# Four graph layers on one core: the order of copy and clear of PSUM banks in the counts

## The chip, the cores and the metric

One NeuronCore of a Trainium2 chip runs one program. The metric is the device time of one execution in microseconds (us). The kernel before was timed three times; one further execution was recorded by the hardware profiler.

## The reference

The program computes four residual graph layers on 6250 nodes of 128 features and 200000 edges, sorted by target. Each layer is fed with `h = relu(layernorm(x))` and adds its result to x:

```
x = x + GIN(h)        # h + sum of h[src] over edges into dst, then two dense layers
x = x + attention(h)  # 8 heads, scores with edge features, softmax per target, then norm
x = x + SAGE(h)       # mean of h[src] over edges into dst, two dense layers
x = x + linear(h)     # sum of edge_weight * h[src], one dense layer
```

Layers one and three sum features over the edges. The kernel does that as a dense product with a matrix of counts: entry (source, target) is the number of edges between the two nodes. The targets are drawn as 6250 times the square of a uniform number, so that low node numbers get many edges and high ones few. Building the matrix of counts is the stage that the change touches.

## The kernel before, in words

The order of the whole is: tables of edges, the counts (`build_counts`), layer one, layer two with the building of the weighted matrix beside it, layers three and four. Each stage ends with a barrier of all engines.

In the counts the 6272 targets (49 blocks of 128) are cut into 784 windows of eight targets. The sums of a window stand in one PSUM bank, 128 partitions by 8 x 49 = 392 numbers. There are eight banks; window w uses bank w mod 8. The edges stand in chunks of 128, and a visit is one chunk taken for one window; there are 2352 visits. Per visit:

- VectorE (`hots`, L676 through `one_hots`) compares keys with a counting row and makes two one-hot matrices, for eight visits per pair of instructions, into a ring of 24 visits (`ba_mov`, `ba_sta`).
- TensorE (`visit`, L713) multiplies the two and adds the product onto the window's bank. The matmul does not reset the bank (`start=False`), so the bank has to be zero before a window's first visit. TensorE waits on `s_clear` for a number read from a table (window plus a constant), and on `s_hot` for the one-hots. Its loop's body holds three groups of eight visits; ahead of each group it loads eight registers.
- ScalarE (`evict_counts`) takes the windows by pairs. It waits on `s_vis` until the pair's last visit is done, copies both banks into the stage in SBUF (L737, `ba_stage`), and clears banks by an ACTIVATE with scale 0 (`clear_pair`, L672), which adds 2 to `s_clear`. Eight pairs are a block; behind them ScalarE issues the DMA of the block to `adj_d` (L743). There are two stage buffers. The loop's body holds two blocks, and a last block stands behind the loop. At the start of a block eight ends of pairs are loaded into registers (`pair_ends`), and `s_store` is waited for.

The copy adds 1 to `s_evict`, and a clear waits for `s_evict` before it overwrites the banks that the copy read. `start` clears all banks once and gives `s_evict` and `s_clear` their first values. Beside the counts GpSimd and SyncE move terms for the attention (L811, L813), and VectorE takes the norm's statistics of x behind its last one-hots.

The weighted matrix is built later by the same class (`evict_weights`): there one bank of 392 is copied (L768), waited for (L769) and cleared (L770, recorded as L665) at a time.

Of the kernel before, what the change touches and what calls it, by code (L numbers as in the profile page):

```python
# [26 lines left out]
WPB = P // WN  # L27
# [30 lines left out]
BANKS = 8  # L58
# [561 lines left out]
class Build:  # L620
# [105 lines left out]
    def evict_counts(self):  # L726

        nc, c, act = self.nc, self.c, self.nc.scalar
        half = WPB // 2

        def block(b, par, turn):
            ends = self.pair_ends(b)
            act.wait_ge(self.s_store[par], 16 * turn + 1)
            for k in range(half):
                act.wait_ge(self.s_vis, ends[k] + self.ring)
                out = self.stage[:, par, :].rearrange("p (h d) -> p h d", d=P)[:, :, 2 * k * WN:2 * (k + 1) * WN].rearrange("p h (t d) -> p t h d", t=2)
                act.copy(out, self.pair_of_banks(2 * k % BANKS).rearrange("p t (h d) -> p t h d", d=WN)).then_inc(self.s_evict, 1)  # L737
                if k:
                    act.wait_ge(self.s_evict, b * half + k + 1)
                    self.clear_pair(2 * (k - 1) % BANKS)  # L740
            act.wait_ge(self.s_evict, b * half + half + 1)
            self.clear_pair((WPB - 2) % BANKS)
            act.dma_start(c.adj_d[bass.DynSlice(b, 1), :, :].rearrange("a p n -> (a p) n"), self.stage[:, par, :]).then_inc(self.s_store[par], 16)  # L743
        with act.Fori(0, NB // 2) as i:
            block(2 * i, 0, i)
            block(2 * i + 1, 1, i)
        block(NB - 1, 0, NB // 2)
        act.wait_ge(self.s_store[0], 16 * (NB // 2 + 1) + 1)
        act.wait_ge(self.s_store[1], 16 * (NB // 2) + 1)
# [1627 lines left out]
```

## Time and profile before

| | us |
|---|---|
| median of 3 runs | 5554.05 |
| lowest, highest | 5548.2, 5557.44 |
| the profiled execution's own time | 5533.22 |
| its span | 5531.4 |
| TensorE matmuls busy | 4526.3 (82%) |
| VectorE busy | 3188.8 (58%) |
| ScalarE busy | 1789.2 (32%) |
| copies of the counts (L737, 392) | 316.8 |
| clears of the counts (L672, 396) | 328.0 |

The span is from the first to the last recorded instruction. Busy times are sums of durations; where two instructions of an engine overlap, the overlap is counted once in the stretches but the durations of single groups are added up. In the timelines an instruction that waited has the idle time and its releaser in brackets.

### The profile page before, as it was taken

The page shows a single profiled execution, that of the slowest core. Times are in us where ns is not written, and L with a number is a line of the kernel's source. Part 1 is how long each engine was busy: PE and PEld are TensorE (multiplying, and loading weights), DVE is VectorE, ACT ScalarE, POOL GpSimd, SP SyncE. Part 2 cuts the span into 40 slices and gives each one's busy share as a digit, 9 for nine tenths or more (in the row PEclk, how much of TensorE's full clock was granted, in tenths as well). Part 3 has the DMA queues.
Part 4 walks back from the last instruction along what each step waited for, and adds up shares of the span by engine and source line. Part 5 has one row for each costly group of instructions (what it writes and reads, how often), then busy time and mean ns, then how long its engine had stood idle before and what let it go on. Part 6 is the DMA issues. An engine that isn't in the chain of part 4 may idle for free. (4 is left out here: it accounts for less than half of the span.)

```text
span 5531.4 us, 87976 instructions
## 1 busy us (share of the span) xinstructions
PE 4526.3 (82%) x25332; PEld 3174.1 (57%) x25333; DVE 3188.8 (58%) x4531; ACT 1789.2 (32%) x3407; POOL 2014.9 (36%) x1926
## 2 busy tenths in 40 slices
PE   6888665565899968888888888888884399999999
PEld 4656332222788844554555455555553388888888
DVE  6323988877211058889998989898985710000000
ACT  2433267889200030112333344455552400001000
POOL 0320026300000007777777777777774400000000
PEclk9989999988999999999999999999995599999999
DMA  8885467755766643445555556666665366669998
GB/s 185 171 155 132 112 220 274 289 232 253 305 279 273 273 144 84 116 135 141 158 159 162 173 179 179 195 200 193 199 205 166 135 280 279 279 255 296 300 293 264
DMA packets 736267, 1150.51 MB, mean 208 GB/s; under 512 B 310041, under 2 KB 659421, under 8 KB 717343
## 3 DMA queue, kind: packets, MB, share of 16 engines
q1 hardware_dynamic: 461057, 653.45, 34.7%
q10 hardware_dynamic: 211504, 349.71, 18.0%
q0 software_dynamic: 63600, 146.16, 10.7%
q8 instruction: 38, 0.62, 0.0%
q14 instruction: 68, 0.56, 0.0%
HBM read 762.49 MB, written 393.26 MB: 209 GB/s over the span
## 5 line engine op out<-in xcount | busy, mean ns | idle before, releaser
L1505 POOL DMA_INDIRECT at_qg<-q_d,at_slot x1616 | 1655.7, 1025 | 496.1 <-issue 492.4
L713 PE MATMUL bw_ps<-bw_mov,bw_sta 128*128 128x392 bf16 x7056 | 1575.2, 346 | 22.2 <-issue 8.3
L1548 PE MATMUL at_psk<-at_kp,at_hot 128*128 x4848 | 613.7, 233 | 338.3 <-DVE at_qg L1626 287.0
L713 PEld LDWEIGHTS bw_ps<-bw_mov,bw_sta 128*128 128x128 bf16 x7056 | 630.9, 101 | 372.2 <-issue 103.8
L1548 PEld LDWEIGHTS at_psk<-at_kp,at_hot 128*128 128x128 bf16 x4848 | 435.6, 100 | 684.9 <-issue 477.9
L713 PE MATMUL ba_ps<-ba_mov,ba_sta 128*128 128x392 bf16 x2352 | 513.8, 365 | 317.9 <-ACT ba_ps L672 136.3
L676 DVE TENSOR_TENSOR ba_mov<-iota,key 128x3136 bf16<-128x3136 f16 x294 | 526.8, 1792 | 132.2 <-PE ba_ps L713 127.0
L713 PEld LDWEIGHTS ba_ps<-ba_mov,ba_sta 128*128 128x128 bf16 x2352 | 242.1, 103 | 589.7 <-issue 475.2
L697 DVE TENSOR_TENSOR bw_sta<-bw_raw,kw 128x1024 bf16<-128x1024 bf16 x882 | 557.5, 688 | 0.0
L1054 PE MATMUL l2agg<-tiles,h 128*128 128x256 f32 (+1 forms) x2450 | 525.0, 376 | 22.4 <-PEq L1075 22.4
L1054 PE MATMUL l3agg<-tiles,h 128*128 128x256 f32 (+1 forms) x2450 | 525.8, 377 | 5.2 <-ACT h L915 5.2
L676 DVE TENSOR_TENSOR bw_mov<-bw_ps,lo 128x3136 bf16<-128x3136 f16 x294 | 524.1, 1783 | 4.4 <-PE bw_ps L713 3.7
L1054 PE MATMUL l0agg<-l0adjt,h 128*128 128x256 f32 (+1 forms) x2450 | 525.1, 376 | 0.3 <-ACT h L915 0.3
L768 ACT COPY xall<-bw_ps 128x392 f32<-128x392 f32 x520 | 252.2, 485 | 795.5 <-PE bw_ps L713 765.3
L1054 PEld LDWEIGHTS l2agg<-tiles,h 128*128 128x128 f32 x2450 | 458.3, 191 | 82.5 <-PEq L1075 22.7
L1054 PEld LDWEIGHTS l3agg<-tiles,h 128*128 128x128 f32 x2450 | 458.7, 191 | 65.5 <-issue 5.3
L1054 PEld LDWEIGHTS l0agg<-l0adjt,h 128*128 128x128 f32 x2450 | 457.4, 191 | 60.5 <-issue 0.5
L1626 DVE TENSOR_TENSOR at_qg<-at_qg,at_psk 128x816 f32<-128x816 f32 (+1 forms) x303 | 274.2, 905 | 240.9 <-DMA at_qg<-q_d,at_slot 213.9
L665 ACT ACTIVATE bw_ps<-iota 128x392 f32<-128x392 f16 x788 | 395.0, 502 | 29.4 <-DMA at_tables<-reg_d 4.7
L737 ACT COPY ba_stage<-ba_ps 128x784 f32<-128x784 f32 x392 | 316.8, 818 | 235.4 <-PE ba_ps L713 221.4
L811 POOL DMA_INDIRECT tv_rows<-ed_d,tv_place x101 | 175.7, 1740 | 457.0 <-DMA edv_d<-tv_rows 295.7
L672 ACT ACTIVATE ba_ps<-iota 128x784 f32<-128x784 f16 x396 | 328.0, 839 | 6.4 <-DMA ba_vend<-vend_d 6.4
(412 smaller groups left out, 3811.8 us busy)
## 6 DMA issues: line engine op xcount, KB each, us to landing
adj_d<-ba_stage ACTq DMA_DIRECT2D x49, 3136.0 KB, 9.1
l0adjt<-adj_d SPq DMA_DIRECT2D x23, 6272.0 KB, 17.2
tiles<-adj_d SPq DMA_DIRECT2D x23, 6272.0 KB, 17.3
tiles<-adw_d SPq DMA_DIRECT2D x23, 6272.0 KB, 20.4
adw_d<-xall ACTq DMA_DIRECT2D x65, 1568.0 KB
adw_d<-bw_stage ACTq DMA_DIRECT2D x33, 1568.0 KB
at_rel<-rel_d SPq DMA_DIRECT2D x101, 512.0 KB
at_qg<-q_d,at_slot POOLq DMA_INDIRECT x1616
```

The lines of the kernel that those rows point to most:

```text
L665: self.nc.scalar.activation(self.ps[:, k * 512:k * 512 + WCOL], self.c.iota2[:].rearrange("p n u -> p (n u)")[:, 0:WCOL], ACT.Copy, scale= ...
L672: self.nc.scalar.activation(self.pair_of_banks(k), self.c.iota2[:].rearrange("p n u -> p (n u)").rearrange("p (t n) -> p t n", t=2), ACT.C ...
L676: return self.nc.vector.tensor_tensor(out, self.iota[:, 0:width, :].unsqueeze(1).to_broadcast([P, UV // 2, width, 2]), pairs(keys).unsquee ...
L697: ins = ve.tensor_tensor(self.sta[:, k, v, :, :], self.raw[:, :, :, :], pairs(c.kw[:, 1 + k, bass.DynSlice(t, UV)]).unsqueeze(2).to_broadc ...
L713: ins = pe.matmul(self.ps[:, bass.DynSlice(place, WCOL)], self.sta[:, k, u // 2, :, u % 2], self.mov[:, u // 2, :, u % 2], start=False, st ...
L737: act.copy(out, self.pair_of_banks(2 * k % BANKS).rearrange("p t (h d) -> p t h d", d=WN)).then_inc(self.s_evict, 1)
L768: act.copy(stage[:, (k % half) * WCOL:(k % half + 1) * WCOL], self.bank(k)).then_inc(self.s_evict, 1)
L811: pool.indirect_dma_start(out=rows[:, k, :], out_offset=None, in_=c.ed_d[:, :], in_offset=bass.IndirectOffsetOnAxis(ap=place[:, g:g + 1], ...
L1054: ins = pe.matmul(ps_agg[par][:, 0:n * P], h[:, hi, :], moving[hi], start=hi == 0, stop=hi == NB - 1 and not own_term, skip_group_check=ow ...
L1505: pool.indirect_dma_start(out=qg[:, ring, b, :], out_offset=None, in_=q_d[:, :], in_offset=bass.IndirectOffsetOnAxis(ap=slot[:, ring, b:b ...
L1548: ins = pe.matmul(ps_k[:, at:at + KW], hot[:, par, sum(ROUNDS[:r]) + u, :], kp[:].rearrange("p j k n -> p (j k n)")[:, bass.DynSlice(place ...
L1626: ve.tensor_tensor(q, q, ps_k.rearrange("p (b n) -> p b n", n=512)[:, :, 0:n * KW], ALU.mult).then_inc(s_kr, 1)
```

## The change

The clear of a pair of banks stands behind the copy of that same pair, and waits for that copy. Before, it stood behind the copy of the next pair, and the last pair's clear behind the loop. The wait ahead of the DMA stays.

```diff
--- before.py
+++ after.py
@@ -735,11 +735,9 @@
                 act.wait_ge(self.s_vis, ends[k] + self.ring)
                 out = self.stage[:, par, :].rearrange("p (h d) -> p h d", d=P)[:, :, 2 * k * WN:2 * (k + 1) * WN].rearrange("p h (t d) -> p t h d", t=2)
                 act.copy(out, self.pair_of_banks(2 * k % BANKS).rearrange("p t (h d) -> p t h d", d=WN)).then_inc(self.s_evict, 1)
-                if k:
-                    act.wait_ge(self.s_evict, b * half + k + 1)
-                    self.clear_pair(2 * (k - 1) % BANKS)
+                act.wait_ge(self.s_evict, b * half + k + 2)
+                self.clear_pair(2 * k % BANKS)
             act.wait_ge(self.s_evict, b * half + half + 1)
-            self.clear_pair((WPB - 2) % BANKS)
             act.dma_start(c.adj_d[bass.DynSlice(b, 1), :, :].rearrange("a p n -> (a p) n"), self.stage[:, par, :]).then_inc(self.s_store[par], 16)
         with act.Fori(0, NB // 2) as i:
             block(2 * i, 0, i)
```

## Rows read from the trace of the kernel before

**Rows 1.** The page's costliest groups: mean ns of one, idle before, what ended it.

```profile
L713 PE MATMUL ba_ps<-ba_mov,ba_sta 128*128 128x392 bf16 x2352 | 513.8, 365 | 317.9 <-ACT ba_ps L672 136.3
...
L676 DVE TENSOR_TENSOR ba_mov<-iota,key 128x3136 bf16<-128x3136 f16 x294 | 526.8, 1792 | 132.2 <-PE ba_ps L713 127.0
...
L737 ACT COPY ba_stage<-ba_ps 128x784 f32<-128x784 f32 x392 | 316.8, 818 | 235.4 <-PE ba_ps L713 221.4
...
L672 ACT ACTIVATE ba_ps<-iota 128x784 f32<-128x784 f16 x396 | 328.0, 839 | 6.4 <-DMA ba_vend<-vend_d 6.4
```

**Rows 2.** Timeline behind the counts (start, duration, instruction, idle and releaser).

```profile
1398.25 0.34 ACT L907 ACTIVATE n_rstd<-n_mv,n_eps 128x49 f32<-128x49 f32 x1 [4.74 <-DMA adj_d<-ba_stage]
```

**Rows 3.** Timeline of VectorE at the start of the counts.

```profile
561.60 1.79 DVE L676 TENSOR_TENSOR ba_mov<-iota,key 128x3136 bf16<-128x3136 f16 x1 [3.54 <-PEq L651]
...
563.91 1.78 DVE L676 TENSOR_TENSOR ba_mov<-iota,key 128x3136 bf16<-128x3136 f16 x1
```

**Rows 4.** Busy time by stretch (columns: length, busy and count by engine, clock, DMA).

```profile
716.90:1000.90 284.00, 170.88 (x814) 82.07 (x815) 238.40 (x204) 194.74 (x256) 141.73 (x81) 0.93 0.71 260
1000.90:1377.10 376.20, 230.63 (x996) 105.44 (x994) 294.03 (x250) 333.65 (x448) 29.02 (x17) 0.87 0.60 251
```

**Rows 5.** The same stretches, copies of the counts (L737) alone.

```profile
716.90:1000.90 284.00, 103.33 (x128) 0.93 0.71 260
1000.90:1377.10 376.20, 181.08 (x224) 0.87 0.60 251
```

**Rows 6.** Timeline of ScalarE, one block of the late stretch.

```profile
1110.30 0.82 ACT L737 COPY ba_stage<-ba_ps 128x784 f32<-128x784 f32 x1
...
1113.85 1.53 ACT L737 COPY ba_stage<-ba_ps 128x784 f32<-128x784 f32 x2 [1.26 <-issue]
1115.26 0.85 ACT L672 ACTIVATE ba_ps<-iota 128x784 f32<-128x784 f16 x1
...
1122.40 0.83 ACT L737 COPY ba_stage<-ba_ps 128x784 f32<-128x784 f32 x1
1123.10 0.85 ACT L672 ACTIVATE ba_ps<-iota 128x784 f32<-128x784 f16 x1
1123.86 0.84 ACT L737 COPY ba_stage<-ba_ps 128x784 f32<-128x784 f32 x1
...
1124.93 0.34 ACTq L743 DMA_DIRECT2D adj_d<-ba_stage  x1
1125.31 0.85 ACT L672 ACTIVATE ba_ps<-iota 128x784 f32<-128x784 f16 x1
1126.28 1.53 ACT L737 COPY ba_stage<-ba_ps 128x784 f32<-128x784 f32 x2
```

**Rows 7.** Timeline of ScalarE, first and last copy of the last block.

```profile
1377.12 1.53 ACT L737 COPY ba_stage<-ba_ps 128x784 f32<-128x784 f32 x2 [0.18 <-PE ba_ps L713]
...
1387.44 0.83 ACT L737 COPY ba_stage<-ba_ps 128x784 f32<-128x784 f32 x1
```

**Rows 8.** Timeline of ScalarE in the weighted matrix: copy, wait, clear.

```profile
2402.13 0.48 ACT L768 COPY xall<-bw_ps 128x392 f32<-128x392 f32 x1 [3.22 <-PE bw_ps L713]
2402.65 0.50 ACT L665 ACTIVATE bw_ps<-iota 128x392 f32<-128x392 f16 x1
```

**Rows 9.** Waits up to 1000.9: us in total, times, longest.

```profile
PE ba_ps L713 <- ACT ba_ps L672: 55.9, 52, 2.4
...
DVE ba_mov L676 <- PE ba_ps L713: 45.2, 39, 2.8
```

**Rows 10.** Timeline of TensorE and ScalarE: bursts of visits and a clear.

```profile
601.11 1.56 PE L713 MATMUL ba_ps<-ba_mov,ba_sta 128*128 128x392 bf16 x8 [0.57 <-DVE ba_sta L676]
...
854.42 1.56 PE L713 MATMUL ba_ps<-ba_mov,ba_sta 128*128 128x392 bf16 x8 [1.79 <-issue]
...
860.17 0.83 ACT L672 ACTIVATE ba_ps<-iota 128x784 f32<-128x784 f16 x1
...
861.32 1.56 PE L713 MATMUL ba_ps<-ba_mov,ba_sta 128*128 128x392 bf16 x8 [1.38 <-ACT ba_ps L672]
```


## The prediction

> **What bounds the kernel now.** I began with the chain of waits. It follows back only from the last instruction, stays inside the fourth layer and says nothing of the counts, so it gives no price here. The costliest groups give the four operations of the counts [rows 1]: VectorE builds one-hots (L676), TensorE multiplies them into PSUM (L713), ScalarE copies a pair of banks (L737) and clears it (L672). Nothing else of size runs on these three engines in that stage, and behind it stands a barrier: the last store has to land before the norm's ACTIVATE at 1398.25 [rows 2]. So what the stage gains or loses, the kernel gains or loses one for one. The stage runs from the first one-hot at 561.60 [rows 3] to the last copy at 1387.44 [rows 7].
>
> Busy time by stretch shows that the bound moves [rows 4]. Up to 1000.9 VectorE leads: 238.4 us of 284.0, ScalarE 194.7. Behind it ScalarE leads: 333.7 of 376.2 (89%), VectorE 294.0, TensorE 230.6. The reason is the data: targets are dense at low node numbers, so an early pair of windows needs many visits of TensorE and a late pair only about four, while ScalarE's work for a pair is always one copy and one clear. The copies counted by stretch say it: 128 in 284.0 us, then 224 in 376.2 us [rows 5]. 224 copies are 28 blocks of eight, 13.44 us each.
>
> How near ScalarE is to its limit there is read from its timeline [rows 6]. Copy to clear is 0.70 (1122.40 to 1123.10), clear to copy 0.76 (1123.10 to 1123.86): 1.46 a pair, less than the 0.83 + 0.85 of the two durations, because each instruction starts before the one ahead of it has ended. A block opens with two copies and no clear between them: third copy at 2.17 (1.41 to the first clear at 1115.26, then 0.76), then five more pairs, 2.17 + 5 x 1.46 = 9.47 from first to eighth copy. From the eighth copy to the first of the next block it is 2.42 where the second block of the loop's body follows (1123.86 to 1126.28) and 3.55 across the loop's edge (1110.30 to 1113.85), mean 2.985. Limit now: 12.45 a block against 13.44 measured, so ScalarE idles only 0.99 us a block. A longer ScalarE block can hide there by less than 1 us.
>
> **The change part by part.** Instructions are the same in number: eight copies, eight clears, one DMA per block. What moves is the clear of pair k, from behind the copy of pair k+1 to behind its own copy.
>
> Added: the clear now waits for the copy straight ahead of it to complete, seven times a block more than before (the eighth clear already did). Queued behind this wait on ScalarE are the clear, the next copy and, at the block's end, the DMA; TensorE waits for the clear, the store for the copy. The counts of before don't show this wait between a copy and its clear (the eighth clear stands behind the seventh). The nearest rows are those of the weighted matrix, where the same code order copy, wait, clear stands: copy at 2402.13 for 0.48, clear at 2402.65 [rows 8]. Start to start 0.52, a duration plus 0.04, no overlap. Here that makes 0.82 + 0.04 = 0.86 in place of 0.70. Bounds: 0.70 if the overlap somehow stays; and 1.06 if the wake-up takes the 0.24 that stands between the eighth copy's end (1124.69) and the DMA's issue at 1124.93 [rows 6]. I take 0.86, the row with the same two kinds of instruction.
> The Trainium skill ("ScalarE: Activation LUTs", What ACT_TABLE_LOAD costs) says that back-to-back ACTIVATEs overlap by about 93 ns; the rows show 0.09 behind a clear and about 0.13 behind a copy. By the page's figure the added time a pair would be 0.093 + 0.04 = 0.13 in place of 0.16, and the late sum about 0.03 x 7 x 29 = 6 us smaller.
>
> Clear to next copy stays 0.76: that copy waits only for TensorE. A saturated pair becomes 0.86 + 0.76 = 1.62, first to eighth copy 7 x 1.62 = 11.34.
>
> The block's end: before, the sequencer waits for the eighth copy, queues the clear (1125.31, behind the clear of pair seven), issues the DMA at 1124.93, loads the next ends and sends the next copy at 1126.28, which is 1.59 behind the eighth copy's end. This path starts from the copy's end in both kernels, so 2.42 and 3.55 stand. One clear fewer lies in that window, but it hid beneath the sequencer: no gain. Bound: if the engine set the pace, 0.76 a block could go; I count none, as 1125.31 + 0.76 is 1126.07, ahead of 1126.28. The store's issue keeps its place behind the eighth copy.
>
> Late stretch: 11.34 + 2.985 = 14.325 a block, x 28 = 401.1, against 376.2: +24.9. The last block: 11.34 against 10.32 (1377.12 to 1387.44) [rows 7]: +1.0. Of the 0.99 idle I leave 0.05 a block, +1: TensorE and VectorE wait with full buffers when ScalarE is the slowest, and they get banks earlier. Late total +27.
>
> Removed: the clear of pair k no longer waits for TensorE to finish pair k+1. TensorE needs the banks of pair k for pair k+4. While it still sums pair k+1 and the banks of k are already read, it could go on before only as far as k+3; now k+4 is open too. Where visits are many and ScalarE has time this can shorten waits. Up to 1000.9 TensorE's waits put down to a clear sum to 55.9 us in 52 [rows 9], but a burst of eight visits shows some 0.6 us ahead of it also where nothing but its own pace holds it (0.57 at 601.11, VectorE named) [rows 10]: 55.9 - 52 x 0.6 = 25 us at most. A real case: the clear at 860.17 lasts until 861.00 and the burst starts at 861.32, 1.38 us idle, 0.8 over the usual [rows 10]; the new order would have cleared earlier. Other gaps, such as the 1.79 at 854.42 that is put down to issue [rows 10], have no clear ending ahead of them; I don't expect them to go. And a shorter wait of TensorE counts only where VectorE then waits for it (45.2 us in 39 up to there) [rows 9]. Between 0 and 25 I take 9, about a third.
>
> Sum: +27 - 9 = +18. Against this execution's own 5533.2 us (span 5531.4) it makes 5551. That execution lies 20.8 below the median of the timed runs, 5554.05, so the forecast for the median is 5554 + 18 = 5572.
>
> **The rivals.**
> *Slack wins (faster).* Place: visits up to 1000.9. Mechanism: one more free pair lets TensorE run through the block's end, where ScalarE stands still for 2.4 to 3.5 us, so VectorE's ring never fills. Price: VectorE's bare pace is 2.31 for eight visits (561.60 to 563.91) [rows 3]; its 204 operations there are 102 batches, 235.6 us in place of 284.0, -48. With +26 behind, -22: 5532. It decides once more than 27 us are saved there, which is more than all waits on clears hold. For it: VectorE idles 46 us. Against: the named excess is 25, and the longest gaps have another releaser.
> *It cancels.* The whole 25 comes back early: +2, 5556. For it: those waits stand in the profile. Against: double counting with VectorE's waits.
> *Idle stays (slower still).* ScalarE keeps its 0.99 us of idle a block: 28 x 0.94 = 26 more, +44: 5598. For it: the granted clock falls to 0.87 in that stretch against 0.93 before it [rows 4], and TensorE at the lower level may be late for pairs. Against: it has more room than before. A wake-up of 1.06 (0.2 x 7 x 29 = +41 on the forecast) belongs to this side.
> *The wait is free.* Copy to clear stays 0.70: nothing lost, -9: 5545. The Trainium skill ("VectorE: DVE Perf Modes", The DRAIN you can't avoid) has it for VectorE that a semaphore behind each op costs nothing extra. Rows 8, on ScalarE, speak against it: 0.52 for an instruction of 0.48.
>
> **How the numbers follow.** Forecast 0.58, idle stays 0.12, it cancels 0.18, slack wins 0.07, free wait 0.05. About 0.2% (11 us) can be told from no change. Slower: 0.12 and 0.54 of the forecast's 0.58, 0.66. Same: 0.04 + 0.18 + 0.03 of the free wait, 0.25. Faster: 0.07 + 0.02, 0.09. The range reaches to the cancelling case below and most of the way to the idle case above: 5553 to 5592.
>
> **What would show it.** ScalarE's timeline after 1000: copy to clear 0.85 to 0.86 (0.70: free wait); clear to copy 0.76; first to eighth copy 11.3 in nearly all late blocks; 2.4 and 3.5 between blocks as before. The late 224 copies in about 400 us. The 128 copies before them in about 275; under 260 means that slack wins. TensorE's waits on a clear should fall early. Blocks well over 14.3 on average late would prove the idle case. I am wrong if the eighth-to-first step changes, or if another stage moves.

## The result and the profile after

Timed in six runs each, the changed kernel has a median of 5578.21 us (5575.21 to 5596.07), the kernel before 5544.44 (5537.16 to 5557.44). The ratio is 1.0057, interval 1.0043 to 1.0071: slower by about 32 us, between 24 and 39.

The profiled execution of the changed kernel took 5596.07 us, 62.9 more than the one before and 18 more than the median of its own runs. Of the 62.9, some 37 lie in the counts and 25.7 in layer two: from the first copy of the weighted matrix (L768 before, L766 after) to the last it takes 2039.5 us before (2130.63 to 4170.18) and 2065.2 after (2169.93 to 4235.14). The medians lie only 33.8 apart, which leaves no room for that second part, so I take it for this one execution's and read only the counts stage from it. Busy time by stretch, cut where block 4, block 20 and block 48 begin (first copy of each); the columns are those of [rows 4]:

```profile
719.30:1003.50 284.20, 170.92 (x809) 81.91 (x809) 238.27 (x203) 206.25 (x256) 136.75 (x77) 0.93 0.72 258
1003.50:1413.10 409.60, 250.95 (x1003) 109.01 (x1003) 295.89 (x251) 353.70 (x448) 36.06 (x21) 0.82 0.56 233
```

The copies of the counts alone, which answer to [rows 5]:

```profile
719.30:1003.50 284.20, 103.65 (x128) 0.93 0.72 258
1003.50:1413.10 409.60, 180.79 (x224) 0.82 0.56 233
```

Blocks 4 to 19 take 284.2 us, as before (284.0). Blocks 20 to 47, again 224 copies, take 409.6 instead of 376.2: +33.4, 14.63 a block. ScalarE is busy for 353.7 us of them (86%, before 333.7 or 89%: the overlap has gone, and small gaps stand in its place). VectorE and TensorE have the same work in a longer time; TensorE's mean granted clock there is 0.82 instead of 0.87. A timeline of ScalarE through one late block, to be set beside [rows 6]:

```profile
1122.30 0.81 ACT L737 COPY ba_stage<-ba_ps 128x784 f32<-128x784 f32 x1 [1.78 <-PE ba_ps L713]
1123.20 0.83 ACT L672 ACTIVATE ba_ps<-iota 128x784 f32<-128x784 f16 x1
1123.96 0.81 ACT L737 COPY ba_stage<-ba_ps 128x784 f32<-128x784 f32 x1
...
1133.93 0.81 ACT L737 COPY ba_stage<-ba_ps 128x784 f32<-128x784 f32 x1
1134.83 0.83 ACT L672 ACTIVATE ba_ps<-iota 128x784 f32<-128x784 f16 x1
1134.98 0.34 ACTq L741 DMA_DIRECT2D adj_d<-ba_stage  x1
1136.33 0.81 ACT L737 COPY ba_stage<-ba_ps 128x784 f32<-128x784 f32 x1 [0.68 <-issue]
```

Copy to clear is 0.90 (1122.30 to 1123.20), clear to copy 0.76. The copy's duration is 0.81, so that there are 0.09 of nothing where there was an overlap of 0.13 before. From first to eighth copy it is 11.63 = 7 x 1.66, and I find 11.63 or 11.64 in every block from 22 to 48: between the first copy and the eighth ScalarE waits for nobody any more. The step from the eighth copy to the next block is 2.40 inside the loop's body (1133.93 to 1136.33) and 3.5 across its edge, as before. The clear, which in [rows 6] stood between other work at the block's end, now ends at 1135.66 and leaves ScalarE idle for 0.68, with "issue" as the releaser: its sequencer is what sets the edge.

The last block and the first instruction behind the store (timeline of ScalarE, beside [rows 2, 7]):

```profile
1413.13 0.81 ACT L737 COPY ba_stage<-ba_ps 128x784 f32<-128x784 f32 x1 [0.77 <-PE ba_ps L713]
...
1424.76 0.81 ACT L737 COPY ba_stage<-ba_ps 128x784 f32<-128x784 f32 x1
...
1434.99 0.34 ACT L905 ACTIVATE n_rstd<-n_mv,n_eps 128x49 f32<-128x49 f32 x1 [6.97 <-DMA adj_d<-ba_stage]
```

11.63 from first to last copy instead of 10.32, and the ACTIVATE that waits for the store starts at 1434.99 instead of 1398.25: +36.7, which the barrier hands on to everything behind.

TensorE and the clears on the page of the profile, and below them the waits up to block 20, beside [rows 1, 9]:

```profile
L713 PE MATMUL ba_ps<-ba_mov,ba_sta 128*128 128x392 bf16 x2352 | 533.4, 373 | 333.5 <-ACT ba_ps L672 149.1
...
L672 ACT ACTIVATE ba_ps<-iota 128x784 f32<-128x784 f16 x396 | 327.5, 828 | 42.4 <-DMA ba_vend<-vend_d 6.5
```

```profile
PE ba_ps L713 <- ACT ba_ps L672: 59.5, 47, 2.4
...
DVE ba_mov L676 <- PE ba_ps L713: 47.6, 43, 2.7
```

TensorE stands before clears for longer over the whole stage (149.1 against 136.3), and up to block 20 the named waits are 59.5 us in 47 against 55.9 in 52. The early gain on which the prediction counted cannot be seen.

### The profile page after: what moved, and what is told of

It is laid out like the page before. It is cut to its first block and busy times, and to the rows that moved or that the text cites. A ratio compares the mean times of both kernels' runs of the same rounds, so it can differ in the third digit from the quotient of the medians.

```text
span 5594.3 us, 87976 instructions
## 1 busy us (share of the span) xinstructions
PE 4562.3 (82%) x25332; PEld 3184.7 (57%) x25333; DVE 3188.6 (57%) x4531; ACT 1825.5 (33%) x3407; POOL 2042.4 (37%) x1926
## 5 line engine op out<-in xcount | busy, mean ns | idle before, releaser
L1503 POOL DMA_INDIRECT at_qg<-q_d,at_slot x1616 | 1681.1, 1040 | 495.8 <-issue 492.4
L713 PE MATMUL ba_ps<-ba_mov,ba_sta 128*128 128x392 bf16 x2352 | 533.4, 373 | 333.5 <-ACT ba_ps L672 149.1
L766 ACT COPY xall<-bw_ps 128x392 f32<-128x392 f32 x520 | 252.3, 485 | 816.0 <-PE bw_ps L713 794.8
L737 ACT COPY ba_stage<-ba_ps 128x784 f32<-128x784 f32 x392 | 316.9, 808 | 200.0 <-PE ba_ps L713 180.5
## 6 DMA issues: line engine op xcount, KB each, us to landing
l0adjt<-adj_d SPq DMA_DIRECT2D x23, 6272.0 KB, 17.3
```

The lines of the kernel that those rows point to most:

```text
L713: ins = pe.matmul(self.ps[:, bass.DynSlice(place, WCOL)], self.sta[:, k, u // 2, :, u % 2], self.mov[:, u // 2, :, u % 2], start=False, st ...
L766: act.copy(stage[:, (k % half) * WCOL:(k % half + 1) * WCOL], self.bank(k)).then_inc(self.s_evict, 1)
L1503: pool.indirect_dma_start(out=qg[:, ring, b, :], out_offset=None, in_=q_d[:, :], in_offset=bass.IndirectOffsetOnAxis(ap=slot[:, ring, b:b ...
```

## The experiments

Theory 1: what the change costs is the overlap of ScalarE's copy with the clear behind it, in the late blocks where ScalarE sets the pace, and the earlier bank is worth nothing. The rivals stand with each run.

Stage times are from the first copy to the last one of the counts in the profiled execution; before it is 800.7 us (130.2 to block 4, 284 to block 20, 376 to block 48, 10.3), in the changed kernel 837.1. Some of these runs were made on chips on which the kernel before itself takes 6725 to 6797 us, because of its second layer: on such a chip the copies of the weighted matrix take 3106.3 us from first to last (run with the later store) instead of 2039.5. The counts stage hardly differs: that same kernel took 785.5 us for it there and 786.8 on a chip on which the kernel before takes 5516. So stages are compared in us, and times by their ratio to runs of the kernel before on the same chip.

**The wait alone.**

```diff
                 if k:
-                    act.wait_ge(self.s_evict, b * half + k + 1)
+                    act.wait_ge(self.s_evict, b * half + k + 2)
                     self.clear_pair(2 * (k - 1) % BANKS)
```

> The order of the kernel before (the clear of pair k-1 behind the copy of pair k), but the clear waits until the copy of pair k is complete, as in the changed kernel. It pays for the wait and gets no bank earlier. Theory 1 (the loss is the copy-to-clear overlap of ScalarE, 0.70 to 0.90 us): copy to clear 0.90, first to eighth copy 0.71 + 0.90 + 0.76 + 5 x 1.66 = 10.67 where ScalarE is full, late blocks 13.65 at least, 28 of them 382 to 400 us against 376 before and 410 in the changed kernel; time +8 to +25 us on before. Rival (the wait is cheap, the loss comes from the new place of the clear, for instance from TensorE and ScalarE meeting in PSUM): copy to clear stays 0.70 to 0.75 and the time within 5 us of before.

Ratio 1.0037 (1.0026 to 1.0048), +25 us; stage 826.4. ScalarE's timeline, and the copies by stretch:

```profile
1100.17 0.83 ACT L672 ACTIVATE ba_ps<-iota 128x784 f32<-128x784 f16 x1
1100.93 0.81 ACT L737 COPY ba_stage<-ba_ps 128x784 f32<-128x784 f32 x1
1101.83 0.83 ACT L672 ACTIVATE ba_ps<-iota 128x784 f32<-128x784 f16 x1
```

```profile
767.40:1055.80 288.40, 102.96 (x128) 0.92 0.71 262
1055.80:1450.00 394.20, 178.34 (x224) 0.87 0.55 233
```

Copy to clear is 0.90 (1100.93 to 1101.83), with no bank freed earlier in exchange. So the wait behind a copy costs 0.2 us wherever it stands. Late blocks take 14.08, 0.4 above their limit of 13.65. The early blocks take 288.4, 4 us more than in either kernel; what that is worth is discussed behind the next runs. The rival (the place of the clear) falls. That this kernel is nevertheless 11 us quicker in the stage than the changed one comes from its block: it opens with two copies and no clear, so that six waits and six clears stand between the first copy and the eighth, and not seven.

**The order by halves of the stage.** The loop is cut in two at block 20, each part with one of the orders:

```diff
...
+        for lo, hi, own in ((0, 10, True), (10, NB // 2, False)):
+            with act.Fori(lo, hi) as i:
+                block(2 * i, 0, i, own)
+                block(2 * i + 1, 1, i, own)
```

(`own` is the changed kernel's order; the second run has `False` and `True` in their places.)

> Blocks 0 to 19 in the order of the changed kernel, blocks 20 to 48 in the order of before. Theory 1: the early part gains nothing and loses nothing, since TensorE there rarely stands before an uncleared bank; blocks 4 to 19 in 284 us as in both kernels, the late 28 blocks in 376, time within 5 us of before. Rival 'slack pays early' (my prediction's own term): 9 us faster than before. Rival 'the order costs early too': 5 to 15 us slower.

> Blocks 0 to 19 in the order of before, blocks 20 to 48 in the order of the changed kernel. Theory 1: the whole loss is here; late blocks 14.6 us each (11.63 from first to eighth copy), 28 of them 409 us, time +33 to +37 us on before, like the changed kernel. Rival (the loss is spread over the stage, or the changed kernel is slow by something outside ScalarE's late blocks): less than +25.

New order early: ratio 0.9997 (0.9987 to 1.0007), stage 798.5. New order late: 1.0043 (1.0029 to 1.0056), +29 us, stage 833.6. Copies by stretch, first of the one, then of the other:

```profile
763.50:1048.20 284.70, 103.67 (x128) 0.94 0.72 262
1048.20:1420.80 372.60, 180.96 (x224) 0.89 0.60 250
```

```profile
763.60:1047.50 283.90, 103.31 (x128) 0.92 0.72 264
1047.50:1454.00 406.50, 180.78 (x224) 0.87 0.54 228
```

The four early figures (284.0 and 283.9 in the old order, 284.2 and 284.7 in the new) lie within 1 us. The late ones differ by the order as before: 406.5 in the new against 372.6 in the old, 33.9. (Both are some 3 us under those of the whole kernels, 409.6 and 376.2: with the loop cut in two, the step across its edge is 3.3 instead of 3.5, 14 times.) All of the loss is in the late blocks. This is theory 1 in both runs, though the new order late fell a little short of what was expected (+33 to +37 us, 409 for the late blocks). Of my own 9 us nothing shows: by the time alone they would lie just at the edge of the interval (0.9987), and it is the length of the early blocks that speaks against them. Single executions scatter, however: the flat copy below, in the new order too, took 288.0 us for these blocks, and the wait alone 288.4. A wait that costs up to 4 us early and a bank that gives as much back is not excluded; a gain on balance of 9 is.

**Copy and clear by bank.** The wait is kept, but the other bank's instruction stands in it:

```diff
...
+                for t in range(2):
+                    act.copy(out[:, t], self.pair_of_banks(2 * k % BANKS)[:, t, :].rearrange("p (h d) -> p h d", d=WN)).then_inc(self.s_evict, 1)
+                for t in range(2):
+                    act.wait_ge(self.s_evict, b * WPB + 2 * k + t + 2)
+                    self.clear((2 * k + t) % BANKS)
```

> The clears stand directly behind their own pair's copies, as in the changed kernel, but copy and clear are cut by bank: copy A, copy B, clear A, clear B, each waiting only for its own copy, so that the wait is covered by the other bank's work. Theory 1 (the wait's lost overlap is the cost): the pair takes about 2 x 0.37 + 2 x 0.41 = 1.56 us instead of 1.66, late blocks about 13.6 us, 28 of them 381, time 0 to +8 us on before, and early blocks as before (284 us). Rival 'slack pays early': the same late, but early blocks 9 us or more shorter, so faster than before. Rival 'an instruction costs more than its elements': the pair 1.66 or more, no better than the changed kernel.

Ratio 1.0037 (1.0023 to 1.0052), +25 us, stage 828.7.

```profile
1200.05 0.90 ACT L738 COPY ba_stage<-ba_ps 128x392 f32<-128x392 f32 x2
1200.80 0.97 ACT L665 ACTIVATE ba_ps<-iota 128x392 f32<-128x392 f16 x2
1201.65 0.91 ACT L738 COPY ba_stage<-ba_ps 128x392 f32<-128x392 f32 x2
```

```profile
766.80:1053.10 286.30, 112.42 (x256) 0.92 0.72 264
1053.10:1452.90 399.80, 206.41 (x448) 0.84 0.55 231
```

The pair takes 1.60 (1200.05 to 1201.65), between 1.56 and 1.66: of the 0.20 that the wait costs 0.06 come back, and twice the instructions eat the rest. The late blocks take 399.8 where 381 was expected. The early blocks (286.3) show no gain from a bank cleared early either. As a repair it fails.

**One clear later still.** If one pair more of free banks is worth nothing, is one fewer?

```diff
-                if k:
-                    act.wait_ge(self.s_evict, b * half + k + 1)
-                    self.clear_pair(2 * (k - 1) % BANKS)
+                if k >= 2:
+                    act.wait_ge(self.s_evict, b * half + k)
+                    self.clear_pair(2 * (k - 2) % BANKS)
```

(the two that are left are cleared at the block's end).

> The order of before, with the clear one copy later still: pair k-2 behind the copy of pair k. ScalarE's work and its waits are those of before (all waits long fulfilled); only the free banks are one pair fewer. Theory 1 says that a pair more of free banks bought nothing in the changed kernel; this asks whether the step below it does cost. If banks don't bind at all: blocks 4 to 19 in 284 us, late 28 in 376, time within 5 us of before. If before stands just where banks begin to bind: early blocks 5 to 20 us longer, late ones 10 us or more longer, time +15 to +40 us.

Ratio 1.0129 (1.0105 to 1.0152), +87 us, stage 892.5. Copies by stretch, and the waits over the whole stage:

```profile
767.60:1070.30 302.70, 103.48 (x128) 0.88 0.69 256
1070.30:1514.10 443.80, 180.42 (x224) 0.76 0.48 203
```

```profile
ACT ba_stage L737 <- PE ba_ps L713: 312.3, 225, 22.1
...
DVE ba_mov L676 <- PE ba_ps L713: 211.4, 170, 3.0
```

Copy to clear is 0.70 and clear to copy 0.76 here, and yet the late blocks need 15.85 us each: ScalarE waits for TensorE (312.3 us, 221.4 before), and VectorE's ring is full (211.4 against 127.0 [rows 1]). Part of it, about 0.5 us in every second block, is a longer edge (2.96 in place of 2.42), since two clears stand there. The loss was more than twice the largest that I had expected. TensorE's waits that name a clear, though, rose only to 141.7 us from 136.3, and its mean granted clock in the late blocks fell to 0.76 from 0.87; how much of the loss is the missing bank itself and how much the lower clock that came with the waiting was not separated. What the edit shows is that the banks do bind, at one free pair fewer than the kernel before has. The next step the other way bought nothing that can be seen.

**What holds the early blocks.** VectorE's bare pace would give 236 us for blocks 4 to 19, ScalarE's limit 199; they take 284. TensorE has long gaps at each block's start [rows 10]. Counted in the trace of the kernel before, blocks 4 to 19 hold 35 gaps of TensorE over 1.3 us, 67.6 us in all; 20 name issue, 13 a clear, 2 VectorE. An estimate from these: with the usual 0.6 taken off each they come to 46.6 us, about what the blocks lie above VectorE's pace. The changed kernel has 35 too, of 69.7 us. Two suspects: the block's store, and ScalarE's standing still at the edge. First the store, cut to 8 of 128 rows, in both orders. These two kernels leave most of the matrix of counts out: behind the stage they write all rows of every block from one and the same buffer, so only the stage is read from them.

```diff
-            act.dma_start(c.adj_d[bass.DynSlice(b, 1), :, :]...., self.stage[:, par, :])...
+            act.dma_start(c.adj_d[bass.DynSlice(b, 1), 0:8, :]...., self.stage[0:8, par, :])...
```

> The order of before, but a block's store carries 8 of the 128 rows; whole rows (of the last block) are written behind the stage, so that only the counts stage (first copy to last copy) is to be read, not the time. Question: what holds the early blocks, if not banks? Theory S (the block's 3.2 MB store slows TensorE's sequencer, whose gaps of 1.8 and 2.4 us follow each block's start): these gaps go, blocks 4 to 19 take 235 to 255 us instead of 284, VectorE becomes the bound. Rival E (ScalarE's standstill of 2.4 to 3.5 us at a block's edge is the cause): gaps and the 284 us stay within 5 us. The edge itself should stay 2.4 and 3.5 if it is sequencer work, and fall if it is slowed by the store.

> The same as the run before it, on the changed kernel's order. With the store's disturbance gone, is there then an early gain from the earlier clear? Theory 1 (ScalarE's chain alone counts): early 16 blocks within 4 us of the tiny-store run in the order of before, late 28 blocks 409 us as with the full store, first to eighth copy 11.63. Rival (slack pays, but the store's stalls hid it): early 16 blocks at least 8 us shorter than in that run.

The edit did not isolate what it should. The DMA of 8 rows holds ScalarE's sequencer longer than that of 128, and the edge rose to 5.7 us (timeline of ScalarE, order of before):

```profile
1114.70 0.87 ACT L737 COPY ba_stage<-ba_ps 128x784 f32<-128x784 f32 x1
...
1115.80 0.52 ACTq L743 DMA_DIRECT2D adj_d<-ba_stage  x1
1116.16 0.88 ACT L672 ACTIVATE ba_ps<-iota 128x784 f32<-128x784 f16 x1
1120.46 1.53 ACT L737 COPY ba_stage<-ba_ps 128x784 f32<-128x784 f32 x2 [3.42 <-issue]
```

With an edge of 5.7 the limits are 9.46 + 5.7 = 15.2 and 11.63 + 5.7 = 17.3 a block, and the blocks from 18 to 47 take just these: 15.13 to 15.22 and 17.26 to 17.34. The first run still took 277.1 for blocks 4 to 19, 7 less than before, although ScalarE stood still 2 to 3 us longer in each, which speaks for the store; with 235 to 255 expected it does not prove it. Its long gaps are 17 in place of 35, one a block, and all begin within 2.5 us behind the small store's issue; they are longer, 51.5 us in all. So the issue of even a small store is followed by a gap, and only those that come later are gone. The second run took 292.1, since ScalarE's limit rules there from block 10 on. Blocks 4 to 9, still above that limit, do answer whether the store hid an early gain: they take 118.4 us in the new order and 118.5 in the old. It hid none there.

Then the store whole, but later, behind the third copy of the next block:

```diff
...
+                if k == 2 and not first:
+                    store(b - 1, 1 - par)
...
```

> The order of before for copies and clears, but a block's store is issued behind the third copy of the next block, not at the block's end. Theory S (the store slows TensorE's sequencer): its gaps of 1.8 and 2.4 us move with the store, to behind the third copy, and stay as many; the blocks stay near 17.7 (early) and 13.4 (late). Rival E (they come from ScalarE standing still at the edge): they stay at the block's start. The edge loses the issue of the DMA: 2.42 and 3.55 become 2.2 and 3.2. Time -8 to +3 us on before.

TensorE's bursts and the store's issue in one block; ScalarE's block starts at 929.01 and the next at 945.32:

```profile
931.66 0.34 ACTq L732 DMA_DIRECT2D adj_d<-ba_stage  x1
...
932.68 1.56 PE L713 MATMUL ba_ps<-ba_mov,ba_sta 128*128 128x392 bf16 x8 [0.99 <-issue]
...
936.17 1.56 PE L713 MATMUL ba_ps<-ba_mov,ba_sta 128*128 128x392 bf16 x8 [1.93 <-issue]
...
939.60 1.56 PE L713 MATMUL ba_ps<-ba_mov,ba_sta 128*128 128x392 bf16 x8 [1.86 <-ACT ba_ps L672]
```

The long gaps, 1.93 and 1.86, now begin 2.6 us behind the store's issue at 931.66, in the middle of the block. In the kernel before, the issue to which the gaps of 1.79 and 2.4 at 854.42 and 858.38 belong is this one, 1.8 us ahead of the first gap's beginning at 852.63:

```profile
850.85 0.34 ACTq L743 DMA_DIRECT2D adj_d<-ba_stage  x1
...
858.38 1.56 PE L713 MATMUL ba_ps<-ba_mov,ba_sta 128*128 128x392 bf16 x8 [2.40 <-issue]
```

In the block behind it the issue is at 947.88 and the gaps are 1.81 and 2.07. Over blocks 4 to 19 the long gaps stay as many, 34 with 68.1 us. Before, 25 of the 35 begin in the first 8 us of a block and the other 10 more than 15 us into it, near the store; with the later store all 34 begin between 3.3 and 11.6 us. In both kernels all begin within 10 us of a store's issue. The gaps go where the store goes, so they belong to the store and not to the standstill, and the changed order of copy and clear left them as they were. Stage 785.5, ratio 0.9992 (0.9981 to 1.0004).

One thing came out otherwise than expected: the step across the loop's edge fell to 2.21 like that inside the body, and not to 3.2. In the late blocks the 28 edges are 20 us shorter in all, but the time from first to eighth copy grows by 12, so that only 8 are gained (368.1 us instead of 376.2). ScalarE sets the pace when its block gets longer, as in the changed kernel; in the order of before, something else stands close behind it. With the ends loaded ahead besides:

> As e9_store_later, and the ends of the second block of the loop's body are loaded ahead of the eighth copy of the first. The edge inside the body becomes engine-bound, 0.70 + 2 x 0.76 = 2.22 at most (already so without it: no gain), the other stays. If ScalarE sets the late pace: 0.2 us per two blocks, within 3 us of e9_store_later. If TensorE sets it: the same time. A candidate for a kernel ahead of both.

Stage 788.9, ratio 0.9989 (0.9976 to 1.0001): the same as without, as expected.

**The edge itself.** Eight blocks in the loop's body, the next ends loaded ahead of the eighth copy, full store at its old place:

```diff
...
+                if k == half - 1 and following is not None:
+                    ahead = self.pair_ends(following)
...
+        with act.Fori(0, NB // 8) as i:
```

> The order of before, but eight blocks in the loop's body (six rounds) and the registers with a block's ends loaded ahead of the eighth copy of the block before it, where ScalarE's sequencer has time. Clears and copies as before. If the block's edge is sequencer work: eighth to first copy 1.5 to 1.7 us (engine-bound: 0.70 + 2 x 0.76 = 2.2 with both clears) in place of 2.42 and 3.55, once in eight 3.5; late blocks from 13.4 to about 12.5, 28 of them 350, 15 to 30 us faster than before. Rival E would also shorten the early blocks by 10 us or more. If TensorE and its clock are close behind ScalarE in the late blocks, the gain is under 10 us.

Ratio 1.0016 (1.0006 to 1.0025), stage 813.6.

```profile
716.70:1008.30 291.60, 103.23 (x128) 0.91 0.71 260
1008.30:1388.90 380.60, 182.34 (x224) 0.90 0.58 242
```

```profile
1174.01 0.83 ACT L740 COPY ba_stage<-ba_ps 128x784 f32<-128x784 f32 x1
...
1182.66 0.81 ACT L740 COPY ba_stage<-ba_ps 128x784 f32<-128x784 f32 x1 [6.36 <-issue]
```

Seven edges of eight fell to 2.21, which is 0.70 and two clears: engine-bound. The eighth, the edge of a body four times as long, cost 8.65 (1174.01 to 1182.66) and in two places about 10. In the late blocks the edges come to 81.3 us in all, against 82.1 before, so that nothing was gained there; with 350 us and a kernel 15 to 30 us faster expected, this forecast failed. Blocks 9 to 14, with no such edge among them, take 105.8 us (821.55 to 927.31), against 105.7 before (815.57 to 921.31), with edges up to 1.6 us shorter: rival E falls a second time.

**Why 0.90 and not 0.86.** The copy writes the stage in pieces of eight numbers. With a copy in the banks' own layout (the counts come out in another order):

```diff
-                out = self.stage[:, par, :].rearrange("p (h d) -> p h d", d=P)[...]
+                out = self.stage[:, par, 2 * k * WCOL:2 * (k + 1) * WCOL].rearrange("p (t n) -> p t n", t=2)
...
+                act.copy(out, self.pair_of_banks(2 * k % BANKS)).then_inc(self.s_evict, 1)
```

> The changed kernel with a copy that writes the stage in the banks' own layout (two rows of 392 in place of pieces of 8 numbers; the counts come out in another order, so the matrix is not the reference's). Question: why copy to clear is 0.90 here, where the weighted matrix's rows gave a duration plus 0.04. Theory W (the last writes of a copy in pieces of 32 bytes come later than its recorded end): copy to clear falls to 0.85 or 0.86, late blocks to 14.3. Rival (two banks or the semaphore make it): it stays 0.90.

```profile
1300.02 0.81 ACT L737 COPY ba_stage<-ba_ps 128x784 f32<-128x784 f32 x1 [1.77 <-PE ba_ps L713]
1300.92 0.83 ACT L672 ACTIVATE ba_ps<-iota 128x784 f32<-128x784 f16 x1
1301.68 0.81 ACT L737 COPY ba_stage<-ba_ps 128x784 f32<-128x784 f32 x1
```

Still 0.90. The pieces are not the reason. One bank of 392 shows 0.52 - 0.48 = 0.04 behind the copy [rows 8] and two banks of 784 show 0.09; what makes the difference stays open.

**A kernel ahead of both.** The later store with before's order was timed once more:

> e9_store_later once more, for its time: its counts stage was 785.5 us from first to last copy against 800.7 before, but on that chip the interval of the time ratio reached from 0.9981 to 1.0004. If the stage's gain is real and nothing gives it back, the time is 8 to 15 us under that of before, ratio 0.9973 to 0.9985. If it was the profiled execution's luck, 0.999 to 1.000.

Median 5505.84 us against 5515.89 on the same chip, ratio 0.9985 (0.9976 to 0.9994); stage 786.8. Copies by stretch:

```profile
712.30:992.00 279.70, 103.51 (x128) 0.90 0.73 266
992.00:1359.20 367.20, 182.14 (x224) 0.92 0.61 254
```

The late 28 blocks take 367.2 instead of 376.2, the early 16 take 279.7. About 14 us of stage and 8 us of time by the ratio (the medians lie 10 apart).

## Why the prediction was right, and what it missed

Direction, place and mechanism were right; the size was +18 and is about +32 (the stage alone +36.4, within the interval). That the forecast of 5572 us came within 6 of the measured 5578.21 is partly luck: it was added to 5554.05, the median of three runs, and the kernel before has 5544.44 over six. The change itself was forecast some 14 us too small.

- *The bound moves, and the late blocks decide.* Shown by the two runs with one order per part: nothing early, all late.
- *Copy to clear 0.70 to 0.86.* Right kind, size off: 0.90. That is 0.04 x 7 x 29 = 8 us. The row that I borrowed was of half the width, and I carried its gap over unchanged. The bounds of 0.70 and 1.06 held it. By the overlap of 93 ns that the Trainium skill gives ("ScalarE: Activation LUTs", What ACT_TABLE_LOAD costs) the cost a pair would have been 0.13, further from the 0.20 that was measured.
- *Clear to next copy 0.76, edges of 2.42 and 3.55.* Held. Of the two signs of being wrong, the eighth-to-first step did not change, and another stage moved in the profiled execution alone.
- *Idle of 0.05 a block left.* Held: 11.63 and a mean edge of 2.95 make 14.58, and the measured block is 14.63. The rival that kept the idle falls. The late term came to 33.4 + 1.3 = 34.7 where I had 27.
- *An early gain of 9 us out of at most 25.* This is the step that failed: "Between 0 and 25 I take 9, about a third." It was nothing (284.2 for 284.0, and 1.5 lost ahead of block 4). I took waits that name a clear as waits for banks. The long gaps of the early blocks follow the store, the 13 that name a clear as well as the 20 that name issue. The case at 861.32 stands behind two of them. The run with the clear one copy later shows that a price of this size for free banks was not absurd; it only does not stand on this side of where the kernel was.
- *A semaphore costs nothing (the free wait).* The run with the wait alone refutes it for ScalarE: 0.90 from copy to clear, and +25 us.

One thing in the prediction is worth keeping: the limit of ScalarE's block was added up from starts, not from durations. By durations (0.83 + 0.85 a pair) the kernel before would have seemed above its limit already, and the wait free.

## What to carry to other kernels

When an instruction has to wait for the one straight ahead of it on the same engine, count the overlap between the two plus the gap that takes its place (here 0.11 to 0.13 and 0.09 us). It is paid in full where that engine sets the pace; put another instruction between them, as the kernel before did. Before freeing a buffer earlier, find out whether anything waits for it: make it free later by one step and earlier by one step, and read both. A wait names what ended last, and not what began the delay; look whether the gap follows something else when that is moved.

## What the runs showed of the hardware

- ScalarE, a PSUM copy and a clear of 784 elements: 0.70 to 0.71 start to start without a wait on the copy, 0.90 with it. By bank (392) the pair of banks takes 1.60.
- With a DMA of 8 rows of 25 KB issued by ScalarE at the block's end, its next copy stood 5.7 us behind the eighth; with one of 128 rows of the same length 2.4 and 3.5.
- A store of 3.2 MB is followed within 10 us by gaps of TensorE of mostly 1.4 to 2.5 us, about two a block, that move with its issue; one of 0.2 MB by a single gap of about 3 us. Why was not found.
- With the store issued at the block's end, the step across the edge of ScalarE's loop is 1.1 us longer than a plain one with a body of two blocks, and 6.4 us or more with eight. With the store issued behind the third copy and a body of two blocks, both steps are 2.21.
